# The first convolution of an ODE step in pairs of row tiles, as 64x64 pieces of the array

## The reference

```python
def odefunc(t, y):
    h = relu(group_norm(y, gn1_w, gn1_b))          # 32 groups of one channel each
    h = concat_conv(t, h, conv1_w, conv1_b)        # 3x3, padding 1; t is a 33rd input channel
    h = relu(group_norm(h, gn2_w, gn2_b))
    h = concat_conv(t, h, conv2_w, conv2_b)
    return group_norm(h, gn3_w, gn3_b)

y = y + dt * odefunc(t, y)                         # six times, dt = 1/6

x = x + dct2(gn(x))
x = x + ode(gn(x))
```

## Time and profile before

| | |
|---|---|
| median of 2 runs | 3934.66 us (3930.53 to 3938.78) |
| profiled execution, span | 3928.6 us (the page gives no other time of it) |
| TensorE busy | 3592.0 us, 21844 matmuls |
| its weight loads | 2039.1 us |
| VectorE busy | 3342.3 us |
| ScalarE busy | 2079.6 us |
| GpSimd busy | 929.9 us |
| granted TensorE clock, mean | 0.970 of full speed |

### The profile page before, as it was taken

One profiled execution on the slowest core, in us unless ns is written; L12 is line 12 of the kernel. 1 busy time (PEld: TensorE's weight loads), 2 busy tenths in 40 slices (PEclk: granted clock), 3 DMA queues, 4 the chain that ended last, 5 costly groups with the idle time before them and its releaser, 6 DMA issues.

```text
span 3928.6 us, 70526 instructions
## 1 busy us (share of the span) xinstructions
PE 3592.0 (91%) x21844; PEld 2039.1 (52%) x21844; DVE 3342.3 (85%) x7423; ACT 2079.6 (53%) x3169; POOL 929.9 (24%) x1589
## 2 busy tenths in 40 slices
PE   3699999999999999999999999999999999999995
PEld 3455554555555555555555555555555555554553
DVE  7688888888888888888888888888888888888885
ACT  0455565555655556555565545655555555655553
POOL 4022212222122221222212231123211322111211
PEclk7899999999999999999999999999999999999998
DMA  3300033113032130311312113311133112231013
GB/s 79 74 17 16 22 45 84 41 60 70 11 84 62 61 58 10 94 63 41 58 42 83 41 41 58 76 49 41 41 58 84 41 41 62 37 83 49 25 41 99
DMA packets 366284, 210.26 MB, mean 54 GB/s; under 512 B 351104, under 2 KB 351472, under 8 KB 364016
## 3 DMA queue, kind: packets, MB, share of 16 engines
q1 hardware_dynamic: 366064, 207.66, 21.2%
HBM read 104.88 MB, written 77.07 MB: 46 GB/s over the span
## 4 chain that ended last, share of the span: by engine, by line
issue 39%; PE 34%; DVE 14%; POOL 10%; ACT 2%; POOLq 1%; DMA 1%; DVEq 0%; SPq 0%; ACTq 0%
PE cps L1246 30%; POOL xn L516 3%; POOL small L479 3%; DVE hb L973 2%; POOL m L513 2%; POOL xn L521 2%; PE xps L1320 2%; DVE hb L976 2%; ACT z L620 2%; DVE bnt L889 1%; POOL hb L496 1%; DVE bnt L896 1%; DVE small L951 1%; DVE bn L1000 1%; DVE ha L976 1%
## 5 line engine op out<-in xcount | busy, mean ns | idle before, releaser
L1246 PE MATMUL cps<-ha,w 128*128 128x399 f16 (+1 forms) x9216 | 1737.6, 342 | 69.7 <-DVE ha L976 64.5
L1246 PE MATMUL cps<-hb,w 128*128 128x448 f16 x8064 | 1645.0, 360 | 0.0
L608 ACT ACTIVATE z<-cps,bias_now 128x448 f32<-128x448 f32 (+2 forms) x1440 | 875.8, 610 | 1128.3 <-PE cps L1246 1100.9
L1246 PEld LDWEIGHTS cps<-ha,w 128*128 128x128 f16 x9216 | 861.0, 99 | 693.6 <-ACT z L608 61.1
L1246 PEld LDWEIGHTS cps<-hb,w 128*128 128x128 f16 x8064 | 748.9, 100 | 678.8 <-issue 41.5
L479 POOL TENSOR_TENSOR small<-small,half 128x1 f32<-128x1 f32 x304 | 190.3, 626 | 2135.6 <-DVE small L942 2133.8
L496 POOL MEMSET hb<- 64x28 f16 (+2 forms) x1152 | 320.5, 278 | 784.6 <-DVE hb L976 666.2
L889 DVE BATCH_NORM_STATS2 bnt<-z 128x6 f32<-128x448 f32 x672 | 413.1, 621 | 94.7 <-ACT z L608 94.7
L620 ACT ACTIVATE z<-z,small 128x798 f32<-128x798 f32 (+1 forms) x384 | 405.8, 1057 | 120.5 <-DVE small L951 120.5
L982 DVE SCALAR_TENSOR_TENSOR y<-z,small,y 128x784 f32<-128x784 f32 x384 | 457.4, 1245 | 6.7
L896 DVE BATCH_NORM_STATS2 bnt<-z 128x6 f32<-128x385 f32 (+1 forms) x768 | 411.4, 546 | 56.9 <-ACT z L608 50.4
(11 more groups left out here) (135 smaller groups left out, 2352.4 us busy)
## 6 DMA issues: line engine op xcount, KB each, us to landing
xa<-x_dram SPq DMA_DIRECT2D x64, 392.0 KB, 7.9
y<-xa SPq DMA_DIRECT2D x16, 1568.0 KB, 7.7
y_dram<-y SPq DMA_DIRECT2D x64, 392.0 KB, 7.1
xs<-in_x_dram SPq DMA_DIRECT2D x31, 784.0 KB, 8.7
x_dram<-x1s SPq DMA_DIRECT2D x30, 784.0 KB, 5.3
fin<-y_dram SPq DMA_DIRECT2D x30, 784.0 KB, 7.8
fin<-x_dram SPq DMA_DIRECT2D x28, 784.0 KB, 8.3
out_dram<-fin SPq DMA_DIRECT2D x28, 784.0 KB, 3.3
```

Source lines behind the costliest of these rows:

```text
L608: nc.scalar.activation(z[slot][:, r0 * width:(r0 + r) * width], cps[i % BANKS][:, 0:r * width], ACT.Identity, bias=bias_now[:, conv:conv + ...
L1246: return pe.matmul(ps, w[:, tap, wl, :], h[:, hl, r0 + a:r0 + a + r, b:b + width], start=(n == 0), stop=(n == len(products) - 1))
```

## The change

`quarter_pair` takes the place of two calls of `tile` for the first convolution. It works on tiles `k` and `k + 1` together, in two halves `d` = 0 and 1 of twelve steps. In each step the tile `k + d` gets its two diagonal quarters, (ix, ox) = (0, 0) and (1, 1), each a matmul with 64 rows and 64 columns of the array. In six of the steps of each half (0 to 5 in the first, 4 to 9 in the second) the other tile gets its two cross quarters (1, 0) and (0, 1). A diagonal quarter has 4 taps x 3 products; a cross quarter has 2 taps that aren't zero, x 3. So a pair has 2 x (12 + 12 + 6 + 6) = 72 matmuls with as many weight loads, where it had 24. Rim products stay as they are but stand at the end of the pair, and both `tile_done` come there. TensorE waits at the start of a pair for the input of both tiles and for both banks, and twice inside a pair on its own semaphore `quarters_done`, so that two rows of pieces don't add into the same place of a bank at once. `pe_gate` is only counted up, behind a wait.

```diff
...
+            def quarter_pair(slot, k, i, n, t, ready, base, pairs, between=()):
+
+                first = needs(0, k - 1) if k else 0
+                if needs(0, k + 1) > first:
+                    pe.wait_ge(ready, base + needs(0, k + 1))
+                if not (isinstance(n, int) and n + i + 1 < BANKS):
+                    pe.wait_ge(evac_done, n + i + 1 - BANKS + 1)
+                pe.sem_inc(pe_gate, 1)
...
+                def quarter(d, ix, ox, n):
+                    taps = [(a, b) for a in range(2) for b in range(2) if 0 <= 2 * b + ix - ox < 3]
+                    wl, hl = products[n // len(taps)]
+                    a, b = taps[n % len(taps)]
+                    return pe.matmul(ps[d][parts[ox]], w1[parts[ix], 2 * a + b, wl, parts[ox]],
+                                     h[parts[ix], hl, r0[d] + a:r0[d] + a + rows[d], b:b + NB],
+                                     start=(ix == ox and n == 0 and d == 0) or (ix != ox and n == 0 and d == 1),
+                                     stop=False)
...
+                for d in range(2):
+                    for m in range(12):
+                        if (k + d, m) in between:
+                            between[k + d, m]()
+                        if d == 1 and m == 0:
+                            pe.wait_ge(quarters_done, 2 * pairs + 1)
+                            pe.sem_inc(pe_gate, 1)
+                        quarter(d, 0, 0, m)
+                        same = quarter(d, 1, 1, m)
+                        if d == 0 and m == 11:
+                            same.then_inc(quarters_done, 1)
+                        if d == 1 and m == 4:
+                            pe.wait_ge(quarters_done, 2 * pairs + 2)
+                            pe.sem_inc(pe_gate, 1)
+                        c = m - 4 * d
+                        if 0 <= c < 6:
+                            quarter(1 - d, 1, 0, c)
+                            cross = quarter(1 - d, 0, 1, c)
+                            if d == 0 and c == 5:
+                                cross.then_inc(quarters_done, 1)
+                rims(0).then_inc(tile_done, 1)
+                rims(1).then_inc(tile_done, 1)
...
-                for k in range(8):
-                    tile(1, 0, k, i, n, s, lo_done, parts - NP, between)
-                    i += 1
+                for k in range(0, 8, 2):
+                    quarter_pair(1, k, i, n, s, lo_done, parts - NP, 4 + 8 * (STEPS * g + s) + k // 2, between)
+                    i += 2
...
```

More of the change, by code:

```diff
@@ L235, in build @@
         rim_zero = sem("rim_zero")
+        pe_gate = sem("pe_gate")
+        quarters_done = sem("quarters_done")
         sp_gate = sem("sp_gate")
@@ L1282, in tile, with rims @@
                 conv_tile(slot, conv, k, i, t, between)
+            def quarter_pair(slot, k, i, n, t, ready, base, pairs, between=()):
[5 more added lines that the diff above has]
+                pe.sem_inc(pe_gate, 1)
+                h = ha[slot][:].rearrange("p l (i j) -> p l i j", j=PADA)
+                rw = rim_w[:, 0, t, :] if isinstance(t, int) else \
+                    rim_w[:, 0, bass.ds(t, 1), :].rearrange("p a n -> p (a n)")
+                r0 = [offsets(TILES1)[k + d] for d in range(2)]
+                rows = [TILES1[k + d] for d in range(2)]
+                ps = [cps[(i + d) % BANKS][:, 0:rows[d] * NB].rearrange("p (i j) -> p i j", j=NB) for d in range(2)]
+                parts = [slice(0, 64), slice(64, 128)]
+                products = [(wl, hl) for wl, hl in ((0, 0), (0, 1), (1, 0))]
+                def quarter(d, ix, ox, n):
[6 more added lines that the diff above has]
+                                     stop=False)
+                def rims(d):
+                    if k + d == 0:
+                        pe.matmul(ps[d][:, 0, :], rw, rim_i[:, RIM1:RIM1 + NB], start=False, stop=False)
+                    if k + d == len(TILES1) - 1:
+                        pe.matmul(ps[d][:, rows[d] - 1, :], rw, rim_i[:, RIM1 + NB:RIM1 + 2 * NB],
+                                  start=False, stop=False)
+                    return pe.matmul(ps[d][:, :, 0:NB:NB - 1], rw,
+                                     rim_i[:, RIMC:RIMC + 2 * rows[d]].rearrange("p (i j) -> p i j", j=2),
+                                     start=False, stop=True)
+                for d in range(2):
[20 more added lines that the diff above has]
+                rims(1).then_inc(tile_done, 1)
@@ L1345, in _ @@
             pe.wait_ge(set_done, 1)
-            for k in range(8):
-                tile(0, 0, k, k, 0, 0, lo_done, 0,
-                     {(6, 0): lambda: statistics(1, IZ, HALVES + 2, pre_done, 4)})
+            for k in range(0, 8, 2):
+                quarter_pair(0, k, k, 0, 0, lo_done, 0, k // 2,
+                             {(6, 0): lambda: statistics(1, IZ, HALVES + 2, pre_done, 4)})
             statistics(1, IY, HALVES + 3, isq_done, 3)
@@ L1411, in step @@
                         between[3 + b, 9] = lambda b=b: dct_columns(b, NBATCH * hn + b)
-                for k in range(8):
-                    tile(0, 0, k, i, n, s + 1 if kind != FIVE else 0, lo_done, parts + 2 * NP, between)
-                    i += 1
+                for k in range(0, 8, 2):
+                    quarter_pair(0, k, i, n, s + 1 if kind != FIVE else 0, lo_done, parts + 2 * NP,
+                                 8 + 8 * (STEPS * g + s) + k // 2, between)
+                    i += 2
             with pe.Fori(0, GROUPS - 1) as g:
```

## The result

The changed kernel takes 4861.66 us (median of 2 runs, 4857.27 to 4866.04) against 3934.66 before: a ratio of 1.236, 95% interval 1.232 to 1.240, or +927 us. The time lies in the range on record and the direction is right, but the forecast was +518, and the sum behind it is wrong in its parts, as the experiments show. That the total fell into the range is in good part luck.

The account below looks back on a forecast made before the run. The prediction took the kernel as TensorE-bound with VectorE close behind. Changes of shape 232, weight loads 219 and waits 67 gave +518 us on the median 3934.66, so 4453 us, 13% slower; range 3930 to 5200.

Parts of the forecast that it names:

- The saving of 0 us: First convolution: each diagonal piece still has 24 products a pair, so a pair takes 4.14 us as before.
- Changes of shape, +232: TensorE switching between quarters and whole array, around pairs and interruptions: 1364 changes at 0.17 us, bounds 0 and 368.
- Weight loads, +219: Cross steps, four loads each: 0.22 us against 0.1725, 0.57 us a pair over 384 pairs; bounds 0 and +1148.
- I take the slow rate and loads one at a time: Cross steps: quarter loads taken at the f32 statistics' rate, 0.055 us for 64 columns, with none overlapping.
- wrong if loads of different pieces overlap: One of three stated signs against the prediction; the others: a free change of shape, diagonal products not starting together.
- Waits, +67: Starts of first convolutions: 44 starts that wait already wait about 1.53 us longer for a second input part.
- cost this at 0: End of a convolution: two tiles to evacuate, some 1.2 us, covered by 1.76 us slack; 115 us without it.
- The clock: Side line: half-idle steps might drop the clock to 1.2 GHz in first convolutions, adding up to 1.6 ms.
- (A): Rival: pieces load and stream independently, changes of shape nearly free; 3920 to 4013 us, not slower; chance 0.14.
- (D): Rival: quarters spread evenly over the array, 18 slots for 24, -397 us, 3540 us; chance 0.04.
- (B): Rival: pieces do not run side by side, as with one-bank writes: 5750 us, or 7100 without overlap; chance 0.08.
- (C): Rival: weight loading becomes the bound of each step, 4850 to 5600 us; chance 0.10.

Follow-up runs that it names:

- quarters_unrolled: The changed kernel with TensorE's inner loop of the four MID steps written out, so it jumps back once a group: 4724.16 us, 1.200.
- whole_pairs: The changed kernel's pairing without its quarters, twelve whole products for each tile: 4633.97 us, 1.176 of the kernel before.

## Why the prediction was right, and where its sum was not

- **The saving of 0 us** on the array is right: a cross step takes 0.173 us. The 24 steps of a pair, as many as its fullest piece has, take 4.14 us.
- **Changes of shape, +232.** A cost is there, and the term is too dear. By rows it is 0.12 us into the whole array and 0.09 out of it around rim products, 0.31 for one interruption. That is 176 us or 0.13 a change for the 0.17 assumed, if all are like these; the busy time grew by 124, and at most 100 reach the time. The Trainium skill (TensorEngine Tiling (Array Packing), Key Properties) calls a change of tiling mode a drain; the 0.12 us on the way in agree with a cost, and are less than the 0.165 that a product's overlap is long.
- **Weight loads, +219: wrong, it is 0.** The step that failed is "I take the slow rate and loads one at a time". The slow rate was that of f32 loads, and the 0.03 us between the rim product and the next one, with loads of 0.10 us, already showed f16 loads side by side. By the prediction's own sign ("wrong if loads of different pieces overlap") this part is refuted: 26 loads passed in 1.04 us, and a cross step took 0.173 us and not 0.22.
- **Waits, +67: the step that failed most.** Pairing alone is +699. I counted the starts of phases and looked for the cover in one place, the statistics at 882.91 to 884.67, and from that slack "cost this at 0". The chain that closes is another: part 2 and part 3 of slot 0's input are split by VectorE behind the statistics of tiles 0 and 2, as the code says (`held`), and a pair both releases those tiles later and asks for those parts sooner. I wrote that "what is queued behind the new waits is only TensorE's own stream", and did not ask what stands behind the old waits of VectorE, whose old wait for a tile's evacuation had become longer by a tile.
- **Code loading:** no term of it. 138 us by quarters_unrolled. The forecast gave the number of quarters, 27648, but not what they do to the loop's length, and it didn't look at the outer loop's jump, 3.7 us in the kernel before.
- **The clock.** I counted it as a side line of half-empty steps. The mean fell as far without any quarter (0.915 in whole_pairs), where the same instructions took 267 us more, and it was 1.00 in a plain pair of quarters.
- **Rivals.** (A) and (D) are out. (B) is out: the diagonal quarters of one bank stream together, 24 quarters in 1.04 us; the rule of the Trainium skill (TensorEngine Tiling (Array Packing), Gotcha 1) doesn't hold here, where the two row groups write different partitions of the bank. (C) gives about the right time, 4850, by the wrong mechanism. That the total lay in the range is luck in so far as it owes much to errors of both signs: 518 = 232 + 219 + 67 forecast, 927 = 699 + 138 + 90 measured.

In one line each, as measured: asking early +207, releasing late +240, both at once another +252, longer loop code +138, and +90 left for the quarters' own time (the rest of 228). The +207 and the +90 hold some code waiting too, up to 27 and 48 us.

## What to carry to other kernels

Leaving out zero blocks by packing an array pays only if the piece with the most work gets less; count the fullest piece first. Where two tiles are joined, look on every other engine at what stands in its list behind the result that is now late, and whether the joined work asks for it: late release and early request cost more together than apart. And count the instructions that a hardware loop's body gains, since a longer body can make each jump back wait for code.

## What the runs showed of the hardware

- A jump back on TensorE took 0.2 us with a body of 476 matmuls and their loads (1027 records), and 3.9 to 7.9 us with 860 or 876 (about 1820 records). With 1677 records it took 0.2 us in one kernel and 4.6 to 4.9 in another, and the outer loop's jump 3.3 to 9.1 us. Written out, the inner loop ran without that wait: 138 us saved in 21 jumps, 6.6 us each, somewhat more than their own rows (5.7).
- The records of 64x64 weight loads last 107 ns, no less than whole ones (97 in the median), but they overlap: 26 in 1.04 us.
- A change from quarters to whole-array products cost 0.12 us, the change back 0.09, around two rim products.
- After a wait of 4.36 us TensorE's granted clock averaged 0.64 for 4.7 us of work and was 1.00 in the next 4.2.
- Two row groups wrote one PSUM bank at once, at different partitions: 24 quarters of 399 columns in 1.04 us.
